# Masking the shared-bank diagonal score tiles by a TensorE product in a causal attention layer

## The reference

```
h = layernorm(x)
q, k, v = h @ Wq, h @ Wk, h @ Wv            # 16 heads of 16 features
s = q . k  per head, -inf where key > query
x = x + (softmax(s / 16) @ v) @ Wo + bo
h = layernorm(x)
x = x + dequantised(h) @ dequantised(weight).T + bias   # blocks of 32 on an FP6 grid
```

## Time and profile before

| | |
|---|---|
| runs of the kernel before | 2033.82, 2026.51, 2031.51 us |
| median | 2031.51 us |
| profiled execution, its own time | 2027.43 us |
| its span, first to last instruction | 2025.7 us |
| mean granted TensorE clock in the span | 0.978 |
| TensorE busy | 1878.4 us (93%) |
| VectorE busy | 1706.3 us (84%) |
| ScalarE busy | 1342.0 us (66%) |
| GpSimd busy | 811.1 us (40%) |

### The profile page before, as it was taken

How to read it: one execution, slowest core, us unless ns; L and a number is a source line. 1 busy time by engine, 2 the same in 40 slices (tenths; PEclk the granted TensorE clock), 3 DMA queues, 4 the chain that set the end, 5 groups by cost and what they waited for, 6 DMA issues and landing times.

```text
span 2025.7 us, 72471 instructions
## 1 busy us (share of the span) xinstructions
PE 1878.4 (93%) x30309; PEld 823.9 (41%) x30309; DVE 1706.3 (84%) x4358; ACT 1342.0 (66%) x2817; POOL 811.1 (40%) x1123
## 2 busy tenths in 40 slices
PE   6799899898999999999999999999999999999994
PEld 2334344343344343534334344434443444444432
DVE  4798897878997979797898979797799899999975
ACT  5357666676776767676676766667666676777660
POOL 4323324231344545454243646444345444211232
PEclk9899999999999999999999999999999999999987
DMA  5442231413132251612414161340613221140000
GB/s 161 124 105 83 60 88 37 116 53 96 41 95 76 72 125 44 142 53 64 114 47 117 38 158 54 79 111 19 161 49 88 68 71 51 39 100 27 11 33 22
DMA packets 173349, 156.51 MB, mean 77 GB/s; under 512 B 43224, under 2 KB 160734, under 8 KB 173022
## 3 DMA queue, kind: packets, MB, share of 16 engines
q1 hardware_dynamic: 173020, 151.88, 27.9%
HBM read 91.89 MB, written 57.02 MB: 74 GB/s over the span
## 4 chain that ended last, share of the span: by engine, by line
PE 56%; DVE 27%; SPq 6%; issue 5%; ACT 3%; POOL 2%; DMA 2%; POOLq 0%; DVEq 0%; ACTq 0%
PE psum L1459 39%; PE psum L1500 15%; DVE max_parts L1202 12%; DVE psum L1197 7%; SPq L677 5%; ACT probs L1015 2%; DVE max_parts L1197 1%; PE psum L1527 1%; ACT acc_sb L1024 1%; PE psum L1519 1%; DVE block_max L1331 1%; DMA qk_scratch<-shop 1%; DVE out_shop L1354 1%; DVE out_shop L1362 1%; DVE stats L1290 1%
## 5 line engine op out<-in xcount | busy, mean ns | idle before, releaser
L1015 ACT ACTIVATE probs<-psum 128x512 f32<-128x512 f32 (+3 forms) x2560 | 1209.9, 538 | 461.3 <-PE psum L1459 448.1
L1202 DVE TENSOR_REDUCE max_parts<-psum 128x1 f32<-128x512 f32 x1536 | 960.1, 682 | 97.8 <-PE psum L1459 93.5
L1459 PE MATMUL psum<-k_rows,q_rows 96*32 96x512 bf16 (+3 forms) x10240 | 851.6, 352 | 65.2 <-DVE max_parts L1197 31.8
L1459 PE MATMUL psum<-q_rows,k_rows 99*32 99x512 bf16 (+3 forms) x10240 | 892.6, 351 | 9.2 <-DMA q_rows<-max_rows 3.9
L1500 PE MATMUL psum<-probs,v_in 128*17 128x512 f32 (+3 forms) x5120 | 591.3, 535 | 15.8 <-ACT acc_sb L1024 15.1
L1197 DVE CUSTOM_DVE_ANT_0 psum<-psum,causal 128x128 f32<-128x128 f32 (+3 forms) x1024 | 475.4, 518 | 97.6 <-PE psum L1459 93.7
L1459 PEld LDWEIGHTS psum<-k_rows,q_rows 96*32 96x32 bf16 x10240 | 280.0, 97 | 475.1 <-DVE max_parts L1202 162.8
L1459 PEld LDWEIGHTS psum<-q_rows,k_rows 99*32 99x32 bf16 x10240 | 282.9, 96 | 402.0 <-ACT probs L1015 209.7
L843 POOL TENSOR_SCALAR_AFFINE_SELECT probs<-probs 128x512 f32<-128x512 f32 x256 | 165.2, 645 | 652.2 <-ACT probs L1015 651.9
L1500 PEld LDWEIGHTS psum<-probs,v_in 128*17 128x17 f32 x5120 | 143.0, 98 | 111.4 <-issue 33.9
L1197 DVE DVE_READ_ACCUMULATOR2_ANT max_parts<- 128x1 f32 x1024 | 145.1, 142 | 0.0
(11 more groups left out here) (157 smaller groups left out, 1205.2 us busy)
## 6 DMA issues: line engine op xcount, KB each, us to landing
q_rows<-qk_scratch SPq DMA_DIRECT2D x384, 64.0 KB, 2.7
k_rows<-qk_scratch SPq DMA_DIRECT2D x384, 64.0 KB, 2.6
qk_scratch<-shop SPq DMA_DIRECT2D x56, 384.0 KB, 3.4
sums_scratch<-acc_sb SPq DMA_DIRECT2D x48, 256.0 KB, 2.3
shop<-in_L_attn_x SPq DMA_DIRECT2D x19, 512.0 KB, 4.4
v_scratch<-shop SPq DMA_DIRECT2D x16, 544.0 KB, 4.3
v_in<-v_scratch SPq DMA_DIRECT2D x64, 136.0 KB, 2.9
out_shop<-in_L_attn_x SPq DMA_DIRECT2D x12, 512.0 KB, 8.7
```

The lines of the kernel that those rows point to most:

```text
L1015: nc.scalar.activation(probs[s % NPROBS][:, h, a:CHUNK], bank[SCORE_BANKS[n % 3]][:, a:CHUNK], ACT.Exp, scale=SCALE).then_inc(probs_ready, 1)
L1202: nc.vector.tensor_reduce(max_parts[k % 2][:, first:first + heads, t % TILES, c], ring_bank(UNIT_USE[n])[:, 0:heads * width] .rearrange("p ...
L1459: ins = nc.tensor.matmul(out[r:r + COLUMNS], weights[:, r:r + COLUMNS], moving, start=start, stop=stop)
```

## The change

Where several heads share a bank, TensorE now opens the bank with the first head's product alone (start only at i = 0) and, after the heads, adds one more product: a bfloat16 identity `identb` times the triangle `maskb` (0 on and below the diagonal, -1e38 above), broadcast over the heads. It writes the last 128 columns of each head: all 512 columns of a four-head bank, twice 128 columns of a two-head bank, again as four matmuls of 32 rows. VectorE then takes such a unit by the same single `tensor_reduce` as a full unit, with one maximum per head. Diagonal units of one head keep the custom instruction; for them the wait on `consts_ready`, so far issued for unit 0 alone, is now issued before each of the 512. GpSimd has two more memsets and two more selects at the start.

```diff
--- before.py
+++ after.py
@@ -435,6 +435,8 @@
             return stack.enter_context(nc.semaphore(name))
 
         ident = sbuf("ident", [P])
+        identb = sbuf("identb", [P], BF16)
+        maskb = sbuf("maskb", [P], BF16)
 
         causal = sbuf("causal", [CHUNK])
         zerob = sbuf("zerob", [CHUNK], BF16)
@@ -814,15 +816,20 @@
 
         @block.gpsimd
         def _(pool):
+            nc.gpsimd.memset(identb[:, :], 0.0)
+            nc.gpsimd.memset(maskb[:, :], 0.0)
             nc.gpsimd.memset(causal[:, :], 0.0)
             nc.gpsimd.memset(half_power[:, :], -0.5)
             for u in range(2):
                 nc.gpsimd.memset(neg_wide[u][:, :], 0.0)
             nc.gpsimd.memset(ident[:, :], 0.0).then_inc(const_step, 1)
             pool.wait_ge(const_step, 1)
-            nc.gpsimd.affine_select(out=ident[:, :], in_=ident[:, :], compare_op=ALU.not_equal, fill=1.0, base=0,
+            for m in (ident, identb):
+                nc.gpsimd.affine_select(out=m[:, :], in_=m[:, :], compare_op=ALU.not_equal, fill=1.0, base=0,
+                                        pattern=[[-1, P]], channel_multiplier=1)
+            triangle = causal[:, CHUNK - P:CHUNK]
+            nc.gpsimd.affine_select(out=maskb[:, :], in_=maskb[:, :], compare_op=ALU.is_ge, fill=MASKED, base=0,
                                     pattern=[[-1, P]], channel_multiplier=1)
-            triangle = causal[:, CHUNK - P:CHUNK]
             nc.gpsimd.affine_select(out=triangle, in_=triangle, compare_op=ALU.is_ge, fill=MASKED, base=0,
                                     pattern=[[-1, P]], channel_multiplier=1).then_inc(consts_ready, 1)
             pool.wait_ge(consts_ready, 1)
@@ -1189,15 +1196,12 @@
                 k, t, c, first, heads = UNITS[n]
                 width = unit_width(n)
                 dve.wait_ge(unit_ready, n + 1)
-                if c == QCS[k]:
-                    if n == 0:
-                        dve.wait_ge(consts_ready, 1)
-                    for i in range(heads):
-                        mine = ring_bank(UNIT_USE[n])[:, i * width:(i + 1) * width]
-                        ins = nc.vector.tensor_tensor_reduce(
-                            out=mine, in0=mine, in1=causal[:, CHUNK - width:CHUNK], scale=1.0, scalar=LOWEST, op0=ALU.add, op1=ALU.max,
-                            accum_out=max_parts[k % 2][:, first + i, t % TILES, c:c + 1])
-                    ins.then_inc(unit_used, 1)
+                if c == QCS[k] and heads == 1:
+                    dve.wait_ge(consts_ready, 1)
+                    mine = ring_bank(UNIT_USE[n])[:, 0:width]
+                    nc.vector.tensor_tensor_reduce(
+                        out=mine, in0=mine, in1=causal[:, CHUNK - width:CHUNK], scale=1.0, scalar=LOWEST, op0=ALU.add,
+                        op1=ALU.max, accum_out=max_parts[k % 2][:, first, t % TILES, c:c + 1]).then_inc(unit_used, 1)
                     return
                 nc.vector.tensor_reduce(max_parts[k % 2][:, first:first + heads, t % TILES, c],
                                         ring_bank(UNIT_USE[n])[:, 0:heads * width]
@@ -1470,7 +1474,11 @@
                 for i in range(heads):
                     ins = by_columns(dst[:, i * width:(i + 1) * width],
                                      q_rows[u][0:ROWS, qc, first + i, t % TILES * P:(t % TILES + 1) * P],
-                                     k_rows[u][0:ROWS, first + i, c * CHUNK:c * CHUNK + width], True, True)
+                                     k_rows[u][0:ROWS, first + i, c * CHUNK:c * CHUNK + width], i == 0, heads == 1)
+                if heads > 1:
+
+                    last = dst[:, :].rearrange("p (h n) -> p h n", h=heads)[:, :, width - P:width]
+                    ins = by_columns(last, identb[:, :], maskb[:, None, :].broadcast_to([P, heads, P]), False, True)
                 ins.then_inc(unit_ready, 1)
 
             def scores(s, h):
```

## The result

The changed kernel takes 2037.05 us (median of 20 runs) against 2030.64 us for the kernel before on the same chip (20 runs). The ratio is 1.0032, with a 95% interval of 1.0022 to 1.0042: 6.5 us slower, with an interval of 4.5 to 8.5 us. A second comparison in the first batch of experiments gave 1.0028 (1.0016 to 1.0041). By the bound of 0.5% that is "the same"; with 20 runs a side it is a small but certain loss. In what follows a ratio is turned into microseconds by 2031 us.

What follows compares the result with a forecast made beforehand. The prediction took TensorE and VectorE to bound the kernel by turns. Added TensorE work 18.3, less VectorE's saving 10.3, plus waits 2.2 made +10.2 us: 2042 us against the median, range 2020 to 2060 us.

Steps and rivals of the forecast that it cites:

- What bounds the kernel: TensorE and VectorE take turns, tied by the ring of four banks; VectorE mostly waits for TensorE at the shared-bank units.
- The prices: Shared-bank units: 0.22 and 0.11 us per added product, 28.2 us on TensorE; plain maxima at 0.61 us save VectorE 41.0 us.
- TensorE's share on the path: Of the added products' 28.2 us on TensorE, 65% was taken to be felt: 18.3 us.
- VectorE's share: Of the 41.0 us saved on VectorE at shared-bank units, 25% was taken to be felt: 10.3 us.
- The second wait: Before the 512 single-head diagonal units, an extra wait costs idle VectorE 0.08 us each time, 2.2 us on the path.
- The sum: Whole kernel: 18.3 - 10.3 + 2.2 = +10.2 us, giving 2042 us against the median.
- VectorE was late after all: VectorE carries its lateness through the shared-bank slots, so most of its saving returns: -20 us, 2011 us; chance 15%.
- TensorE pays all: In the shared-bank slots all added TensorE work is felt and VectorE's saving turns idle: +28 us, 2060 us; chance 20%.
- the gap in the output: Two-head products write two runs with a gap, so might take 0.22 us each: +19 us, 2051 us; chance 8%.
- that the saving isn't there: The plain maximum over several heads takes as long as VectorE's custom instructions did: +20 us, 2052 us; chance 5%.
- Signs named ahead: Changed profile: TensorE's chain share above 56%, VectorE's idle time ahead of the new maxima rising, its busy time some 41 us lower.
- the 0.08 us delay: Idle VectorE should start a single-head diagonal unit 0.08 us later than a plain one, because of two waits.

Runs made afterwards that it cites:

- pe_only: Changed kernel with the added mask products on TensorE, but VectorE still using custom instructions for every head of shared banks: 2043.91 us, ratio 1.0069 to the kernel before.
- one_wait: Changed kernel with the wait for the constants issued only before the first unit: 2037.77 us, ratio 1.0040 to the kernel before.
- the first two runs: Changed kernel with only the added products on TensorE, 2043.91 us; then with only the plain maximum on VectorE, no product, constants wait before first unit only, 2018.85 us.

## Why the prediction was right, and where its sizes were off

The forecast was +10.2 us, at the border of 0.5%; measured are +6.5 us. The range held it, but it was 40 us wide; the sign was right; and it is within 0.5%, to which the prediction gave 36% against 49% for more than that, so the likelier of the two didn't come. What supports the mechanism are the two halves measured alone, not the closeness of the sum, in which errors of opposite sign met.

- *What bounds the kernel.* Right. Two engines take turns, and VectorE usually waits at the units in question. Taking 39 us from VectorE gave 11, and adding 28 to TensorE cost 14.
- *The prices.* Right: 0.22 and 0.11 us for the products. The plain maximum saves 36.5 us of VectorE's busy time against 41.0 forecast. In the changed kernel the next plain maximum follows a four-head or two-head one after 608 ns in the middle case (41 and 34 of them), where 0.61 us was forecast.
- *TensorE's share on the path*, taken as 0.65 for 18.3 us, was mis-sized: pe_only measures 0.50, 14.0 us. The interval of 0.38 to 0.62 leaves the chain's own 60% possible and excludes the step from there to 0.65, which I took because VectorE waits in these slots. What hides the other half isn't shown: that TensorE also waits for ScalarE and the DMAs, and the added work falls there, would fit, but no run tests it.
- *VectorE's share*, taken as 0.25 for 10.3 us: 0.27, 11.0 us. The figure is met, but the interval of 0.18 to 0.35 holds the chain's 34% too, so that lowering it was right isn't shown.
- *The second wait*, 2.2 us: wrong, its cost is nothing that can be seen, as one_wait and the 24 ns show. The step that failed is taking `attend` for a like case. There the late semaphore is the wait that stands alone in the queue; here it is the constants', long since raised, and VectorE starts 24 ns after its release as with one wait. The 94 ns row told of the order of two waits and not of their number.
- *The sum.* With the measured terms it is 14.0 - 11.0 + 0 = +3.0 us, 3.5 us short of the 6.5 measured. Whether that is a joint effect of the two halves or spread, the intervals don't tell; I had no term for one. Against the forecast of 10.2 us, TensorE's share was 4.3 us too dear and the second wait 2.2, VectorE's gain 0.7 too small, and the 3.5 us go the other way. That the forecast missed by only 3.7 us is in part luck.
- *The rivals.* "VectorE was late after all" (-20 us) and "TensorE pays all" (+28 us) both fall with the first two runs; the gap in the output falls with the row at 519.95 us; that the saving isn't there falls with the maxima of 686 ns.
- *Signs named ahead.* The chain's share of TensorE rose from 56% to 61%, which by the spread of 58% to 65% between equal kernels, and by pe_only's 56%, proves little; idle time ahead of the new maxima from 69.9 to 94.7 us. The product alone does 14.1 us of that, VectorE's earliness 10.2. Only the 0.08 us delay didn't come.

## What to carry to other kernels

When two engines share a ring of buffers and both are busy most of the time, here for 93% and 84%, moving work between them pays only if the amount taken away times its share on the path exceeds the amount added times its own; here 41 x 0.27 stood against 28 x 0.50, so a trade that was favourable by the busy times was a loss. Run the two halves of such a trade alone: each half's share comes out of one run. And ask first whether the work must be done at all: dropping the mask from a maximum that only guards a softmax's range gave 23 us where moving it lost 6. That holds for inputs like these, whose masked scores don't lie so far above the others that the exponentials vanish.
